# An early-fusion transformer block on one core: the second group's image input issued in the middle of the weight loads

## What is computed

```python
# tok: patch embedding, layer norm, positions; ff, attention over 64 tokens, ff
x = einsum('bchpwq,dcpq->bhwd', patches(input), patch_w) + patch_b
x = layernorm(x) + positions
identity = x
x = attention(ff(x)) + identity            # 12 heads of 16
x = ff(x) + x
h = concatenate([x, txt], axis=1)           # 64 + 32 = 96 tokens
# attn: a gated causal convolution, attention (12 heads of 16), a feed-forward
a = layernorm(h); a = a + ssm(ln1(a)); a = a + attn(ln2(a)); a = a + gelu_ff(ln3(a))
h = h + a
# ffn: attention with 12 heads of 64, normed q and k, top-2 gates per head
h = h + gated_attention(layernorm(h))
```

## Time and profile before

| | us |
|---|---|
| median of 3 runs | 673.8 (671.29 to 675.58) |
| the profiled execution | 679.45 |
| its span | 677.7 |
| PE busy | 578.7 (85%) |
| DVE busy | 435.3 (64%) |
| ACT busy | 293.1 (43%) |
| mean granted TensorE clock | 0.919 |

### The profile page before, as it was taken

One profiled execution on the slowest core, in us unless ns is written; L12 is line 12 of the kernel. 1 busy time (PEld: TensorE's weight loads), 2 busy tenths in 40 slices (PEclk: granted clock), 3 DMA queues, 4 the chain that ended last, 5 costly groups with the idle time before them and its releaser, 6 DMA issues.

```text
span 677.7 us, 10708 instructions
## 1 busy us (share of the span) xinstructions
PE 578.7 (85%) x4137; PEld 405.6 (60%) x4137; DVE 435.3 (64%) x879; ACT 293.1 (43%) x392; POOL 59.3 (9%) x56
## 2 busy tenths in 40 slices
PE   4600999898888989999998999999996889999786
PEld 3400865674656766566776776577584564774465
DVE  4000356776984488488684675787863978865983
ACT  0200154436342255465561454574733456542553
POOL 0000123000021003020101012021000020010000
PEclk9655899999599799999997899999997899998989
DMA  4598000100000000010000000000000000000000
GB/s 113 151 224 235 1 1 1 54 1 6 1 1 1 0 2 1 1 48 2 6 1 20 1 1 2 0 1 1 1 1 18 1 1 0 2 1 18 0 1 18
DMA packets 13442, 16.01 MB, mean 24 GB/s; under 512 B 6683, under 2 KB 10958, under 8 KB 13006
## 3 DMA queue, kind: packets, MB, share of 16 engines
q1 hardware_dynamic: 11790, 14.12, 8.0%
q10 hardware_dynamic: 1600, 1.18, 0.5%
HBM read 14.11 MB, written 1.18 MB: 23 GB/s over the span
## 4 chain that ended last, share of the span: by engine, by line
issue 38%; PE 32%; DVE 12%; SPq 8%; POOL 5%; ACT 4%; DMA 1%; POOLq 0%; ACTq 0%; DVEq 0%
PE ps L643 8%; SPq L554 5%; PE ps L647 5%; PE ps L919 3%; PE ps L977 3%; PE ps L742 2%; DVE smax L1576 2%; DVE pr L1578 2%; POOL side_wide L1798 2%; PE ps L967 1%; DVE psum L1587 1%; DMA x_in<-in_xT 1%; DVE pr L1599 1%; PE ps L702 1%; PE ps L801 1%
## 5 line engine op out<-in xcount | busy, mean ns | idle before, releaser
L1576 DVE TENSOR_REDUCE smax<-ps 96x12 f32<-96x1152 f32 x32 | 43.2, 1349 | 29.6 <-PE ps L967 19.0
L702 PE MATMUL ps<-side_in,x_in 128*128 128x192 f32 x96 | 21.9, 396 | 43.1 <-DMA x_in<-in_xT 43.1
L1253 ACT ACTIVATE pr<-pr 96x1152 f32<-96x1152 f32 x28 | 32.6, 1163 | 45.7 <-DVE pr L1578 45.7
L702 PEld LDWEIGHTS ps<-side_in,x_in 128*128 128x128 f32 x96 | 20.2, 238 | 45.0 <-issue 39.5
L643 PE MATMUL ps<-w_cqkv,side_c 128*128 128x512 f32 (+1 forms) x102 | 44.9, 571 | 1.2 <-DVE pr L1578 1.2
L977 PE MATMUL ps<-w_ident,pr 96*96 96x96 f32 x336 | 35.3, 259 | 7.8 <-DVE pr L1599 6.2
L1386 DVE TENSOR_TENSOR a_emb<-ps,w_patch_b 128x384 f32<-128x384 f32 x3 | 1.7, 558 | 61.9 <-PE ps L702 61.9
L1259 ACT ACTIVATE pT<-ps 96x1152 f32<-96x1152 f32 x28 | 31.5, 1125 | 20.5 <-PE ps L977 20.4
L977 PEld LDWEIGHTS ps<-w_ident,pr 96*96 96x96 f32 x336 | 30.2, 132 | 15.0 <-issue 6.1
L1587 DVE TENSOR_REDUCE psum<-pr 96x12 f32<-96x1152 f32 x28 | 37.5, 1341 | 2.2 <-ACT pr L1253 2.2
L1578 DVE TENSOR_TENSOR pr<-ps,smax 96x1152 f32<-96x1152 f32 x28 | 37.9, 1353 | 1.0
(11 more groups left out here) (363 smaller groups left out, 1307.1 us busy)
## 6 DMA issues: line engine op xcount, KB each, us to landing
x_in<-in_xT SPq DMA_DIRECT2D x3, 768.0 KB, 4.7
b_kB<-in_cqkv SPq DMA_DIRECT2D x1, 1152.0 KB
w_cqkv<-in_cqkv SPq DMA_DIRECT2D x2, 567.0 KB
w_cqkv<-in_cqkv SPq DMA_DIRECT2D x1, 864.0 KB
out<-side_c ACTq DMA_DIRECT2D x3, 288.0 KB, 2.3
x_in<-in_xT SPq DMA_DIRECT2D x3, 256.0 KB, 4.5
side_in<-in_patchT SPq DMA_DIRECT2D x3, 192.0 KB, 3.4
side_tff<-in_tok_ff SPq DMA_DIRECT2D x1, 576.0 KB, 6.7
```

Source lines behind the costliest of these rows:

```text
L702: m = pe.matmul(t[:, tile * D:(tile + 1) * D], x_in[:, j, tile * 128:(tile + 1) * 128], w_patch[:, j, :], start=(j == 0), stop=(j == KP - 1))
L1253: act.activation(w.y.pr[:, s % 2, :], w.y.pr[:, s % 2, :], ACT.Exp, scale=head ** -0.5)\
L1576: dve.tensor_reduce(mx, t, AX.X, ALU.max).then_inc(w.S[stage + "_sub"], 1)
```

## The change

SP issues the DMA that fills `x_in` for the second group directly behind the loads of `w_tproj` and ahead of the first group's text, in place of behind `w_cproj`. The wait for `early_filled_a_em` moves with it. In "loop" nothing is changed; SP's part of the unit `a_em` now does nothing outside of it.

```diff
@@ -582,6 +582,8 @@
             for rows in (slice(0, HC), slice(HC, HC + 1)):
                 sp.dma_start(w_tproj[rows, :, 0:D], tok_proj[rows]).then_inc(loads["tproj"], 16)
                 sp.dma_start(w_tproj[rows, :, D:256], tok_proj[rows, :, 128:D]).then_inc(loads["tproj"], 16)
+            sp.wait_ge(S["early_" + filled("a_em")], upto("early_" + filled("a_em"), 0))
+            sp.dma_start(x_in[:, :, :], xT[1]).then_inc(S["x_in"], 16)
             text(0, S["early_txt_in"])
             sp.dma_start(last_row[:, :], cqkv[HC - 1:HC, 1, :].to_broadcast([128, 3 * NH * HD2]))\
               .then_inc(loads["cqkv"], 16)
@@ -603,14 +605,10 @@
                 sp.sem_inc(S[name], PER_GROUP[name])
 
             def a_em(w, _):
-                if w.chain == "d":
-                    return
-                if w.section == "pre":
-                    sp.wait_ge(S["early_" + filled("a_em")], upto("early_" + filled("a_em"), 0))
-                else:
+                if w.section == "loop":
                     sp.wait_ge(w.S[filled("a_em")], w.upto(filled("a_em"), w.a - 1))
                     sp.wait_ge(w.S[filled("c_qt")], w.upto(filled("c_qt"), w.c - 1, 2))
-                sp.dma_start(x_in[:, :, :], xT[w.group]).then_inc(w.S["x_in"], 16)
+                    sp.dma_start(x_in[:, :, :], xT[w.group]).then_inc(w.S["x_in"], 16)
```

## The result

The changed kernel takes 642.58 us (median of 4 runs, 639.32 to 645.32), against 672.54 us for the kernel before (4 runs, 670.92 to 675.58): a ratio of 0.9548, with a 95% interval of 0.9487 to 0.9608. Measured again later, it took 645.76 us (4 runs, 640.81 to 648.91) against 674.36, a ratio of 0.957 (0.9519 to 0.962). So the gain is 29 to 30 us, and the changed kernel scatters more than the one before: its ten executions lie between 639.32 and 653.47, the fifteen of the kernel before that were measured with them between 670.92 and 676.86.

What follows compares the result with a forecast made beforehand. The kernel's start was taken as bound by loads (PE waits 38.0 us for x_in), the rest by PE and its neighbours. 33.0 us earlier less 0.2 for late DVE gives 32.8; 673.8 - 32.8 = 641.0 us, range 636 to 648.

Steps and rivals of the forecast that it cites:

- the prediction's own signs of being wrong: Forecast wrong if a_em to a_wc.0 is not the 31.2 us of before, or the clock stays at half beyond 40 us.
- When x_in lands: SP's x_in load, issued at 29.6, lands 4.7 us later at 34.3; ends of the range 34.0 and 36.8.
- What that is worth on PE: On PE, a_em starts at about 34.4 in place of 67.37, 33.0 us earlier, and the work behind moves as one piece.
- What lies under the loads: 33 us of work now runs beside 226 GB/s of loads; no slowing was counted.
- rival 2: PE runs short of code, its instruction fetches slow under the loads; gain 22.8 us, time 651.0; chance 0.04.
- The clock at a_em: PE's clock falls in the pause before a_em and stays at half for the same 4.7 us, 15 matmuls.
- What is late next: DVE's a_wc.0 comes up at 65.6 and waits for w_cproj, landing 65.9 (65.4 to 67.2); 0.2 us put in the sum.
- the cover of 0.87 us: DVE idles 0.87 us between a_wc.0 and the reciprocal; a_wc.0 may be that late, until 66.4, at no cost.
- rival 1: Weights become the wait: w_cproj lands at 72.6, a_wc.0 is 6.2 us past its cover, gain 26.8, time 647.0; chance 0.07.
- The one instruction in the moved piece that waits for late loads: Claimed that DVE's a_wc.0 alone, in the work moved 33.0 us earlier, waits for late loads.
- Rival 3: Slower than before: last of cqkv and cproj lands after 99.2, holding DVE; at 110 it gives 684.6; chance 0.02.
- 4 (nothing moves): PE's wait at a_em goes over into another that ends at the same time; 673.8 us; chance 0.01.

Runs made afterwards that it cites:

- e2: The changed kernel with the x_in DMA and its wait moved back behind the loads of cqkv, in_proj and out_proj, ahead of w_qkv; 663.1 us.
- e9: The changed kernel, unaltered, measured again beside others; 645.76 us, its profiled execution 647.85.
- e7: The changed kernel with only SP's five plain semaphore increments moved to the start of SP's program; median 649.03 us, profiled execution 642.88.
- e10: The kernel of e7 (changed kernel, SP's five increments first) measured again beside e9; 644.42 us.
- e1: The changed kernel with the loads of w_cgate, last_gate and w_cproj moved ahead of the sixteen w_qkv loads; 639.43 us.
- e12: The changed kernel with DVE's a_wc.0 moved behind d_o.1, other engines' orders kept; 643.28 us.
- e3: The changed kernel with the x_in DMA and its wait moved further forward, behind tok_ff1 and ahead of tok_ff2; 643.72 us.
- e4: e3 with the loads of w_cgate, last_gate and w_cproj also moved ahead of w_qkv; 644.92 us.
- e11: e6 with DVE's a_wc.0 moved behind d_o.1, other engines' orders kept; 637.14 us.
- e5: e4 with SP's five plain semaphore increments moved from behind all loads to the start of SP's program; 636.77 us.
- e6: e5 with the loads of w_cgate, last_gate and w_cproj moved ahead of those of cqkv too; 634.46 us.
- e8: The kernel before with only the w_cgate, last_gate and w_cproj loads moved ahead of w_qkv, x_in left last; 676.63 us.

## Why the prediction was right, step by step

The time lay within the range and 1.6 us from the forecast, and the mechanism is the forecast one. That it came so close has some luck in it. The gain is 30.0 us and the forecast had 32.8, 2.8 too many; 1.3 us of this were given back because the kernel before has 672.54 as a median of four executions, and the forecast subtracted from 673.8, a median of three. And one of the prediction's own signs of being wrong came up: the distance from a_em to the first instruction of a_wc.0 is 33.04 us and not the 31.2 of before. The steps below say where this comes from.

**When x_in lands**: right. 4.6 us after the issue at 29.60; the sum had 4.7, from the quiet rows. The formula of the Trainium skill (DMA: Bandwidth & Descriptors, section "Anatomy of one DMA — SWDGE (gpsimd) path"), fitted for the other path, makes an estimate of 3.8 us, and is short here too. e2 shows the other end, 21.1 us behind a full queue, far beyond the 7.2 that the prediction took for a full one. The profile of the kernel before had this already, in the load of w_out (`side_out` in the view: KB, us to landing), issued at 36.47; the prediction's "up to 12.6 us to land" passed over it:

```profile
side_out<-in_out_proj SPq DMA_DIRECT2D x1, 288.0 KB, 19.2
```

PE's wait was 6.1 us and not 5, because in this execution PE was done with d_f1.0 1.1 us earlier than before; that changed nothing for a_em.

**What that is worth on PE**: right, 32.99, and the whole row of work did move as one piece; every row of PE, DVE, ACT and POOL between 34.38 and 65.4 stands 32.89 to 32.99 us ahead of its old place.

**What lies under the loads**: right. The same gelu took 2.30 us beside 203 GB/s of loads as it had without, and PE was busy without a gap from 41 to 66.5, though two packets of instruction fetches came before 67 us, where before there was none (the view of DMAs until 67 us):

```profile
q8 instruction: 2, 0.03, 0.2%
```

So rival 2 is out. The prediction's other comparison was loose: 0.45 us for 256 columns and 0.31 for 192 are not the same rate but some 9% apart. a_em settles it, 15 matmuls in 4.70 us beside the loads and in 4.63 without.

**The clock at a_em**: right. It fell as before, a_em ran at half for the same 4.7 us, 15 matmuls, and from 39.1 to 41 the mean was 0.95.

**What is late next**: the place was right, the size too small. The term was 0.2 us, from a landing of w_cproj at 65.9. It landed at 61.45 + 5.9 = 67.35, just past the 67.2 that was the upper end, because SP issued it 2.3 us later than before (59.16), where the prediction had only the issue of x_in, 0.34 to 0.37 us. 0.4 us are that, 0.6 more were lost by the issues between it and w_qkv, and the sixteen w_qkv issues took 16.56 us in place of 15.33. So it landed 1.9 to 2.0 us later than before, the whole of the 1.8 that was the upper end; the gap of the DMA engines at 50 to 54 made up nothing (their share there is 0.65, as it was 0.64). DVE ran L1456 32.90 us earlier than before and the reciprocal 31.99 us, so with the cover of 0.87 us used up this cost 0.9 us in the first profile. In e9 the two are 34.25 and 30.57, a loss of 3.7, in which the slow subtraction has 1.7. The prediction's rival 1 is thus true in kind, at a seventh of its 6.2 us in the first profile and, with the slow subtraction taken off, a third of it in e9.

**What the sum had not**: a late DVE makes PE pause, and behind the pause PE's clock was at half for a time, in each of the four profiles with this order of loads and of DVE (the changed kernel, e7, e9, e10). From the reciprocal to the scores the lead shrinks from 31.99 to 30.35 in the first profile, 1.6 us, and from 30.57 to 25.22 in e9, 5.3 us. With it, 33.0 - 1.0 - 1.6 = 30.4 us, and the medians show 672.54 - 642.58 = 30.0. e1, without the lateness, has neither; e12 neither (its scores are 32.5 us ahead of the kernel before, which is nearly the whole 33.0).

**"The one instruction in the moved piece that waits for late loads"**: false as put. There was a second, L1456 by way of SP's increments. It had 3.5 us to spare and so didn't touch the forecast, but it is what e3 and e4 ran into. It could be read ahead of the result in the order's waits: a semaphore of two chains that SP raises too.

Rival 3 (slower) and 4 (nothing moves) are out: DVE's wait was 1.7 to 2.7 us, not 33, and x_in landed in 4.6.

## What to carry to other kernels

A load that one engine waits for with everything queued behind it belongs at the first quiet place of the queue behind which its buffer is free; its price is its landing there, 4.6 us, and not its size, as the same DMA took 21.1 us eight microseconds later. Moving it hands the critical path to the next absolute time in the program, so list them all beforehand: the last landing that any engine waits for, and also plain increments that stand behind the loads in the issuing engine's program. Where a wait for a late load stands in the middle of an engine's order, put it behind the work that doesn't need it: e11 and e12 did so, and DVE's lateness went from the path in both traces, if not visibly from the medians.

## What the runs showed of the hardware

**DVE and POOL hold each other up.** In the changed kernel DVE's late subtraction (both inputs in SBUF) falls onto POOL's products, which it did not before, where it ended at 101.72 and POOL began at 101.97. In the first profile DVE started first, at 68.13: it took 2.54 us and POOL's two products 4.35 in place of 2.89. Before the change and after it:

```profile
101.97 2.89 POOL L1798 TENSOR_TENSOR side_wide<-attn,w_mask 128x1024 f32<-128x1024 f32 x2 [10.67 <-ACT attn L1151]
```

```profile
69.07 4.35 POOL L1796 TENSOR_TENSOR side_wide<-attn,w_mask 128x1024 f32<-128x1024 f32 x2 [10.68 <-ACT attn L1149]
```

In e9 POOL started first, at 67.72, and DVE, 0.12 us behind it, took 4.25 us; POOL's two products took 5.27, so both engines paid. The Trainium skill says so (SBUF — State Buffer, section "Who interferes with whom"): a DVE instruction with two SBUF inputs contends with a GpSimd instruction that reads SBUF, the shared pair of ports is an exclusive lock, and the order of issue decides who blocks. The traces agree, in both orders. A shift of a fraction of a us decided whether DVE paid, and with DVE on the path that was worth 1.7 us in e9. It is no single case: in e5, e6, e11 and e12, where a_wc.0 begins while POOL is at its products, its first instruction, of one column, took 0.76 to 1.02 us in place of 0.16. In e5 and e6 that put the subtraction 1.4 us later, on the path. POOL and DVE in e5:

```profile
60.75 2.88 POOL L1795 TENSOR_TENSOR side_wide<-attn,w_mask 128x1024 f32<-128x1024 f32 x2 [10.67 <-ACT attn L1148]
```

```profile
61.64 1.02 DVE L1698 TENSOR_TENSOR ones_row<-w_ident 128x1 f32<-128x1 f32 x1 [4.21 <-DMA w_cproj<-in_cproj]
```

**The clock fell behind short pauses, but not every time.** At this one place PE pauses twice, ahead of L835 and ahead of L631. Where the pauses were 0.81 and 0.67 us long, the clock stayed at full behind them in the kernel before, e1 and e12, and fell for a few us in e2, e8 and e11. Where the first was 1.64 us or longer (the changed kernel, e7, e9, e10, and e3, e5 and e6), the clock was at half behind the two every time. Among the first four it stayed low for longest in e9 and e10: the mean of e10 from 70 to 84 us is 0.63.

```profile
70.00:84.00 14.00, 11.32 (x30) 6.71 (x30) 6.64 (x7) 2.54 (x4) 6.97 (x4) 0.63 0.00 1
```

So a late DVE goes with the fall in every profile and with the longest ones. These are single executions; how often the clock falls with either pause was not counted, and that the pause alone decides it is not shown.

**Where a transfer stands in the queue counts for more than its bytes.** x_in took 4.6, 7.2 and 21.1 us at three places of the same queue, its own bytes unchanged, and w_cproj took 5.9 us as the last load and 21.0 us ahead of w_qkv (e1).
